# First expert layer of a graph kernel: transposes and node products at other places in TensorE's order, LayerNorm rows remade by ScalarE, an output norm in fused operations

## The chip, the core and the metric

The kernel runs on one core of a Trainium2 chip. The metric is the device time in microseconds of one execution, the median of three runs. A core has TensorE (PE in the profile, its weight loads PEld), VectorE (DVE), ScalarE (ACT), GpSimd (POOL) and SyncE (SP), which issues DMAs. Each engine runs its own instructions in the order in which they are written, and engines wait for one another by semaphores.

## What is computed

A graph layer and an expert layer, each twice, over 6250 nodes of 256 numbers. The part that matters is the first expert layer, and the first step of the second graph layer behind it:

```python
def _L0_ffn_ref(x, Wr, br, W1, b1, W2, b2, gamma, beta):
    ...
    h = jax.nn.gelu(jnp.einsum('nd,edf->enf', xf, W1) + b1[:, None, :], approximate=False)
    y = jnp.einsum('enf,efd->end', h, W2) + b2[:, None, :]
    ...
    out = jnp.einsum('ne,end->nd', w_dense, y).reshape(B, S, D)
    out = _layer_norm(out + x, gamma, beta)
    return out

def _L1_gnn_ref(x, W, edge_index):
    ...
    h = x @ W
    ...

x = x + _L0_gnn_ref(_layernorm(x, axis=-1), ...)
x = x + _L0_ffn_ref(_layernorm(x, axis=-1)[None], ...)[0]
x = x + _L1_gnn_ref(_layernorm(x, axis=-1), L1_gnn_W, edge_index)
```

All nodes share one choice of two experts, so the two experts together are one network with 1024 hidden units. Its input is LN1, the LayerNorm of x. Its result plus LN1 is normed with gamma and beta (the output norm) and added to x. LN2, the LayerNorm of that new x, is multiplied by the 256x256 matrix of the second graph layer, which gives the node products h.

## The kernel before

The 6250 rows are 50 tiles of P = 125 rows, taken GT = 2 at a time, so there are G = 25 groups g of N = 250 rows. Every engine has a function `ffn0(g)` that says what it does in its round g, and `in_turns` calls it for 0 to 24: the first few and the last few written out, the others in a hardware loop of two rounds a turn. Nothing but the order in these functions and the semaphores sets the order of the work. A float32 matrix product is made of three products of rounded parts: every operand is split into a high part and what is left (`h_hi`, `h0_lo`, `xB_hi`, `xB_lo`).

For one group the work runs through the engines like this:

- TensorE, `hidden0(g)`: the first products, in four quarters of 12 matmuls (L2088 to L2090), into four PSUM banks.
- ScalarE, `hidden0(g)`: two Gelu activations for each quarter (L794), and the high part `h_hi` of the quarter before (L787).
- GpSimd, `hidden0_lo(g)`: the low part of each quarter (L1028), four subtractions.
- TensorE, inside `ffn0(g)`: the second products, 48 matmuls (L2111 to L2113).
- VectorE, `ffn0(g)`: remakes the LN1 rows out of x with the kept mean and rstd (L1531), adds the bias `b2B` (L1535) and the products (L1538); statistics of y (L1406, L1411, L1413); GpSimd's `root` gives rstd (L998, semaphores `s_vB` and `s_rB`); then the norm (L1545), times gamma (L1547), plus beta (L1549), onto x (L1551); statistics of x; a second `root` (`s_v2`, `s_r2`); the LN2 rows `xh` (L1559).
- TensorE, `T2(g)`: four transposes of `xh` (L2067). ScalarE, `T2_copy(g)`: the copy into SBUF (L772). TensorE, `H(g)`: the node products (L2076).
- ScalarE, `h_copy(g)`: four activations (L780, L781) that write `h_row` and the high half of `h_part_r`. GpSimd, `h_lo_part(g)`: one subtraction (L1032) for the low half. SyncE, `store_h(g)`: the two stores to memory, of 256,000 bytes (L538) and 512,000 bytes (L539).

`h_row` and `h_part_r` exist once. So `h_copy(g)` waits until the stores of group g-1 have landed (the semaphores `h_written0` and `h_written1`, `s_hw` in the code):

```python
def h_copy(g, s):
    act.wait_ge(s_hm, g + 1)
    if not (isinstance(g, int) and g == 0):
        for k in range(2):
            act.wait_ge(s_hw[k], g * 16)
```

The rounds overlap. In round g TensorE does `T2(g-2)`, `hidden0(g+1)`, `H(g-2)` and the second products of g; ScalarE does `T2_copy(g-2)`, `hidden0(g+1)`, `x_hi(g+3)` and `h_copy(g-2)`; GpSimd does the root for the output norm of g-1, the four subtractions of g+1, the root for LN2 of g-1, and `h_lo_part(g-2)`. After the last round come two more `T2` and `H`, two `h_copy` and two `h_lo_part`. The next stage starts when the last stores and three loads behind them on SyncE's queue have landed.

Of the kernel before, what the change touches and what calls it, by code (L numbers as in the profile page):

```python
# [109 lines left out]
def build(nc, a, out):  # L110
# [3 lines left out]
    with ctx:  # L114
# [90 lines left out]
        b2B = b2A  # L205
        gamma = sb("gamma", [P, D])
# [196 lines left out]
        s_vB, s_rB = sem("lnB_var"), sem("lnB_rstd")  # L403
        s_v2, s_r2, s_x2, s_t2, s_t2e = sem("ln2_var"), sem("ln2_rstd"), sem("ln2_rows"), sem("ln2_T_in_psum"), sem("ln2_T_in_sbuf")
# [218 lines left out]
        def _(act):  # L623
# [139 lines left out]
            act.wait_ge(s_wbc, 1)  # L763
            act.wait_ge(s_wB, 96)
# [46 lines left out]

            for k in range(2):
# [142 lines left out]
        def _(pool):  # L955
# [78 lines left out]
            def ffn0(g, s=None):  # L1034
# [119 lines left out]
        def _(dve):  # L1154
# [299 lines left out]
            ln1_rows(G - 1, (G - 1) % 2)  # L1454

# [66 lines left out]
            def ffn0(g, s=None):  # L1522
# [15 lines left out]
                v.tensor_tensor(y, ps[0:P, 4 + s, :].rearrange("p (t d) -> p t d", t=GT), z, ALU.add).then_inc(s_oBe, 1)  # L1538
# [778 lines left out]
```

## Time and profile before

| | us |
|---|---|
| three runs | 3173.44, 3174.09, 3176.77; median 3174.09 |
| the profiled execution: its time, its span | 3175.92, 3174.1 |
| first expert layer's loop and its end (about 1496 to 1932 us of the span) | 436 |
| of the span busy: PE, PEld, DVE, ACT, POOL | 72%, 66%, 64%, 27%, 65% |
| mean granted clock of TensorE over the span | 0.826 |

A timeline row gives the start in us from the span's start, how long it took in us, the engine, the line, the operation, output and inputs, how many instructions stand in the row, and in brackets how long the engine had been idle and what ended that. A row of several instructions reads from the first one's start to the last one's end; matmuls and activations overlap their neighbours by a little, so the distance from start to start is what one costs. A row of a line "A:B" is a stretch of time with the busy time of each engine (and instructions), the granted clock as a share of full speed, the busy share of the DMA engines and GB/s.

### The profile page before, as it was taken

What the parts mean: (1) busy time and instruction counts of PE and PEld (TensorE: products, weight loads), DVE (VectorE), ACT (ScalarE), POOL (GpSimd) and SP (SyncE); (2) the same over time, 40 slices, a digit from 0 to 9 for tenths busy, and PEclk for the clock granted to TensorE, in tenths of its full rate; (3) what the DMA queues carried; (4) which work ended last, traced back from release to release, by engine and by line L of the source; (5) the groups of instructions that cost most, each with busy time, mean ns of one, the idle gap of its engine ahead of it and who ended that gap; (6) DMA issues with size and microseconds to landing.
All of it is one profiled execution on the core that took longest, in us unless ns stands there. A gap on an engine that the chain in (4) does not pass through costs nothing.

```text
span 3174.1 us, 49123 instructions
## 1 busy us (share of the span) xinstructions
PE 2284.6 (72%) x14349; PEld 2096.1 (66%) x14350; DVE 2044.1 (64%) x3305; ACT 863.4 (27%) x2246; POOL 2067.8 (65%) x1707
## 2 busy tenths in 40 slices
PE   0000047779899995997889984777887877798997
PEld 0000036668888885775889873666676767798997
DVE  8889976732323332465788876765665567488987
ACT  0000012210000000132545442344454421354543
POOL 5777877777777775010555545567788742488886
PEclk9999998865555555698999996899999895699999
DMA  6543345455444452122011114566777753423231
GB/s 202 151 115 94 81 124 152 146 163 123 114 114 117 113 136 71 50 77 66 20 49 51 51 61 139 140 165 187 193 197 190 192 146 112 86 63 84 63 90 33
DMA packets 341517, 358.60 MB, mean 113 GB/s; under 512 B 209280, under 2 KB 248560, under 8 KB 341125
## 3 DMA queue, kind: packets, MB, share of 16 engines
q1 hardware_dynamic: 209538, 196.84, 21.3%
q0 software_dynamic: 105984, 93.52, 13.0%
q10 hardware_dynamic: 25853, 66.46, 6.8%
q8 instruction: 75, 1.23, 0.2%
q14 instruction: 67, 0.55, 0.1%
HBM read 234.90 MB, written 122.85 MB: 113 GB/s over the span
## 4 chain that ended last, share of the span: by engine, by line
PE 35%; POOL 25%; issue 15%; DVE 13%; DMA 4%; DVEq 4%; SPq 4%; ACT 1%; another core or an unknown queue 0%; POOLq 0%; ACTq 0%
POOL sorted L989 18%; PE ps L1984 13%; PE ps L2133 4%; POOL h_lo L1028 3%; PE ps L2033 3%; PE ps L2152 3%; PE ps L2143 3%; DVEq L1596 2%; DVE hT L1606 2%; DVE yb L1874 2%; PE ps L2011 2%; POOL rstd L998 1%; SPq L595 1%; SPq L594 1%; DMA big<-x_rows,idx_a 1%
## 5 line engine op out<-in xcount | busy, mean ns | idle before, releaser
L1064 POOL DMA_INDIRECT mid<-h_rows,idx_a x400 | 485.5, 1214 | 172.5 <-issue 113.7
L1984 PE MATMUL ps<-big 128*128 128x65 f32 x2380 | 528.6, 419 | 87.5 <-issue 49.7
L1984 PEld LDWEIGHTS ps<-big 128*128 128x128 f32 x2380 | 514.0, 331 | 103.2 <-issue 102.4
L1361 DVE COPY mid<-big 128x28 f32 (+1 forms) x85 | 22.6, 266 | 448.2 <-PE ps L1984 306.8
L998 POOL TENSOR_TENSOR rstd<-var,neg_half 125x2 f32<-125x2 f32 (+1 forms) x75 | 63.2, 843 | 373.1 <-DVE var L1413 373.0
L989 POOL DMA_INDIRECT sorted<-yb,idx_a x200 | 239.6, 1198 | 83.9 <-issue 60.5
L989 POOL DMA_INDIRECT sorted<-wk,idx_a x200 | 238.1, 1191 | 60.9 <-issue 60.9
L989 POOL DMA_INDIRECT sorted<-xh,idx_b x200 | 237.9, 1190 | 60.9 <-issue 60.6
L989 POOL DMA_INDIRECT sorted<-mid,idx_b x200 | 237.9, 1190 | 60.9 <-issue 60.3
L2152 PE MATMUL ps<-adj,h_in_r 128*128 128x304 f32 (+3 forms) x980 | 244.2, 376 | 38.3 <-issue 36.1
L1606 DVE TENSOR_TENSOR hT<-ps,mid 128x608 bf16<-128x608 f32 (+3 forms) x245 | 255.1, 1041 | 0.1
L1897 PE MATMUL ps<-ones,ends 125*49 125x1 f32 x16 | 2.6, 230 | 343.5 <-DVE ends L1214 343.5
L2143 PE MATMUL ps<-hT,mid 128*128 128x288 bf16 (+3 forms) x637 | 146.2, 335 | 130.7 <-DVE hT L1606 108.7
L1897 PEld LDWEIGHTS ps<-ones,ends 125*49 125x49 f32 x16 | 1.9, 177 | 347.2 <-DVE ends L1214 332.0
L2133 PEld LDWEIGHTS ps<-mid 125*128 125x128 f32 x1600 | 218.8, 217 | 2.3 <-issue 1.5
L2152 PEld LDWEIGHTS ps<-adj,h_in_r 128*128 128x128 f32 x980 | 173.8, 212 | 68.6 <-issue 53.1
L2133 PE MATMUL ps<-mid 125*128 125x96 f32 x1600 | 216.9, 298 | 1.2 <-issue 1.2
L847 ACT ACTIVATE adj<-ps 128x304 fp32r<-128x304 f32 (+3 forms) x245 | 111.1, 457 | 373.4 <-PE ps L2143 276.3
L1598 DVE TENSOR_TENSOR mid<-hT,mid 128x2 f32<-128x2 f32 (+3 forms) x294 | 45.8, 161 | 217.0 <-PE ps L2143 107.5
L1107 POOL TENSOR_TENSOR h_lo<-x,h_hi 128x500 fp32r<-128x500 f32 x128 | 166.3, 1328 | 24.8 <-ACT h_hi L913 22.4
L1028 POOL TENSOR_TENSOR h_lo<-ends,h_hi 128x500 fp32r<-128x500 f32 x100 | 142.4, 1440 | 50.5 <-ACT h_hi L787 48.1
L1362 DVE TENSOR_TENSOR big<-ps,big 128x1792 f32<-128x1792 f32 x85 | 171.5, 2018 | 0.0
(333 smaller groups left out, 6534.4 us busy)
## 6 DMA issues: line engine op xcount, KB each, us to landing
h_in_r<-h_parts SPq DMA_DIRECT2D x245, 256.0 KB
big<-sorted ACTq DMA_DIRECT2D x85, 469.0 KB
sorted<-hT SPq DMA_DIRECT2D x73, 469.0 KB
mid<-in_L_ffn_w SPq DMA_DIRECT2D x16, 1024.0 KB
hid_x<-hT ACTq DMA_DIRECT2D x25, 500.0 KB
mid<-hid_x SPq DMA_DIRECT2D x25, 500.0 KB
h_parts<-h_part_r SPq DMA_DIRECT2D x25, 500.0 KB
mid<-h_rows,idx_a POOLq DMA_INDIRECT x400
```

The lines of the kernel that those rows point to most:

```text
L847: act.activation(adj[:, s, 0:w], ps[:, 2 + s, 0:w], ACT.Copy).then_inc(s_adje, 1)
L989: nc.gpsimd.indirect_dma_start(sorted_rows[c], bass.IndirectOffsetOnAxis(to_row[k][:, i:i + 1], 0), va[k][:, i, :], None).then_inc(s_put[k ...
L1028: nc.gpsimd.tensor_tensor(h0_lo[:, s, m, :], h0_whole[:, s, m, :], h_hi[:, s, m, :].bitcast(f32), ALU.subtract).then_inc(s_hBlo, 1)
L1064: nc.gpsimd.indirect_dma_start(mg4[:, s, i, :], None, h_rows, bass.IndirectOffsetOnAxis(idx4[:, s, i:i + 1], 0)).then_inc(s_gk[s], 16)
L1107: nc.gpsimd.tensor_tensor(h_lo[:, s, m, :], h_whole[:, m, :], h_hi[:, s, m, :].bitcast(f32), ALU.subtract).then_inc(s_hlo, 1)
L1362: v.tensor_tensor(node_hot[:, s % 2], lo_near.unsqueeze(1).to_broadcast([BR, GA, BR]), rows2[:, s, :, CW:CW + 1].to_broadcast([BR, GA, BR] ...
L1606: v.tensor_tensor(dst_sel[:, s, 0:n * w].rearrange("p (k w) -> p k w", w=w), near[:, 0:w].unsqueeze(1).to_broadcast([BR, n, w]), dst_rel[: ...
L1984: i_ = mm(banks[:, bass.ds(o_, CW)], node_hot[:, s % 2, i, :], rows2[:, s, i, 0:CW], start=False, stop=True, skip_group_check=True)
L2033: i_ = mm(ps[0:P, 4 + s, t * D:(t + 1) * D], hT[:, s, m, t * P:(t + 1) * P], wA2[:, m, :], start=(m == 0), stop=(m == 3))
L2133: i_ = mm(ps[:, 4 + s, c * WN:(c + 1) * WN], mg4[:, slot, i, c * 128:(c + 1) * 128], onto[:, slot, i, :], start=(i == 0), stop=(i == HW - 1))
L2143: i_ = mm(ps[:, 2 + s, 0:w], node_sel[:, s, k, :], dst_sel[:, s, k * w:(k + 1) * w], start=(k == 0), stop=(k == n - 1))
L2152: i_ = mm(ps[:, c, 0:w], h_in_r[:, slot, k, c * 128:(c + 1) * 128], adj[:, s, 0:w], start=(first and k == 0), stop=(last and k == 1))
```

## The change

It has five parts, all in the rounds of `ffn0`.

1. TensorE does `T2(g-2)` behind `hidden0(g+1)` rather than ahead of it, and `H(g-2)` behind the second products of g rather than ahead of them.
2. ScalarE's order follows: `hidden0(g+1)`, `T2_copy(g-2)`, the new `ln1_again(g+1)`, `x_hi(g+3)`, `h_copy(g-2)`.
3. ScalarE remakes the LN1 rows: `ln1_again` makes two Identity activations with the rstd as scale and minus mean times rstd as bias (`ln1_bias`, set once by VectorE in the storage of `cnt`), into `yb`. VectorE only adds `b2B` there, and then the products.
4. VectorE adds beta to x before it waits for the root; after it come two fused operations of 125x256, (y - mean) * gamma, and two, z * rstd + x, in the place of L1545 to L1551.
5. GpSimd does its subtraction for the stores one round later and in another place: `h_lo_part(g-3)` between the second and the third quarter of `hidden0_lo(g+1)`, where `h_lo_part(g-2)` came last in the round.

```diff
@@ ScalarE
+            def ln1_again(g, s):
+                if not (isinstance(g, int) and g < 2):
+                    act.wait_ge(s_yr, g - 1)
+                for t in range(GT):
+                    n = bass.ds(g * GT + t, 1)
+                    i_ = act.activation(yb[:, s, t, :], x[:, n, :].rearrange("p a d -> p (a d)"), ACT.Identity, bias=ln1_bias[:, n], scale=rstd1[:, n])
+                i_.then_inc(s_z, 1)
...
+                if not (fixed and g == G - 1):
+                    hidden0(g + 1, 1 - s)
                 if not (fixed and g < 2):
                     T2_copy(g - 2, s)
                 if not (fixed and g == G - 1):
-                    hidden0(g + 1, 1 - s)
+                    ln1_again(g + 1, 1 - s)
                 if not (fixed and g >= G - 3):
                     x_hi(g + 3, 1 - s)
                 if not (fixed and g < 2):
                     h_copy(g - 2, s)
@@ GpSimd
                 if not (fixed and g == G - 1):
-                    hidden0_lo(g + 1, 1 - s, range(4))
+                    hidden0_lo(g + 1, 1 - s, range(2))
+                if not (fixed and g < 3):
+                    h_lo_part(g - 3)
+                if not (fixed and g == G - 1):
+                    hidden0_lo(g + 1, 1 - s, range(2, 4))
                 if not (fixed and g == 0):
                     root(s_v2, s_r2, g, rstd2[:, 1 - s, :], var2[:, 1 - s, :])
-                if not (fixed and g < 2):
-                    h_lo_part(g - 2)
@@ VectorE
-                for t in range(GT):
-                    v.tensor_scalar(z[:, t, :], x[:, bass.ds(g * GT + t, 1), :].rearrange("p a d -> p (a d)"),
-                                    mv1[:, bass.ds(g * GT + t, 1), 0:1].rearrange("p a d -> p (a d)"),
-                                    rstd1[:, bass.ds(g * GT + t, 1)], ALU.subtract, ALU.mult).then_inc(s_dve, st.up())
-                settle()
-                v.tensor_tensor(z, z, wide(b2B), ALU.add).then_inc(s_dve, st.up())
+                dve.wait_ge(s_z, g + 1)
+                v.tensor_tensor(y, y, wide(b2B), ALU.add).then_inc(s_dve, st.up())
...
+                v.tensor_tensor(xs, xs, wide(beta), ALU.add).then_inc(s_dve, st.up())
                 dve.wait_ge(s_rB, g + 1)
                 for t in range(GT):
-                    v.tensor_scalar(z[:, t, :], y[:, t, :], mv[:, s, t, 0:1], rstd[:, s, t:t + 1], ALU.subtract, ALU.mult).then_inc(s_dve, st.up())
-                settle()
-                v.tensor_tensor(z, z, wide(gamma), ALU.mult).then_inc(s_dve, st.up())
-                settle()
-                v.tensor_tensor(z, z, wide(beta), ALU.add).then_inc(s_dve, st.up())
-                settle()
-                v.tensor_tensor(xs, xs, z, ALU.add).then_inc(s_dve, st.up())
+                    i_ = v.scalar_tensor_tensor(z[:, t, :], y[:, t, :], mv[:, s, t, 0:1], gamma[:, :], ALU.subtract, ALU.mult)
+                i_.then_inc(s_yr, 1)
...
+                    v.scalar_tensor_tensor(row, z[:, t, :], rstd[:, s, t:t + 1], row, ALU.mult, ALU.add).then_inc(s_dve, st.up())
@@ TensorE
-                if not (fixed and g < 2):
-                    T2(g - 2, s)
                 if not (fixed and g == G - 1):
                     hidden0(g + 1, 1 - s)
                 if not (fixed and g < 2):
-                    H(g - 2, s)
+                    T2(g - 2, s)
...
                 i_.then_inc(s_oB, 1)
+                if not (fixed and g < 2):
+                    H(g - 2, s)
```

The order of the instructions on GpSimd shows part 5. Here are the rounds that are written out behind the loop, before the change; `h_lo<-ends,h_hi` is a quarter of `hidden0_lo`, `h_part_r<-wk,h_part_r` is `h_lo_part`, the waits lnB_var and ln2_var belong to the two roots:

```order
L998 TENSOR_TENSOR rstd<-var,neg_half 125x2 [waits lnB_var]
L1028 TENSOR_TENSOR h_lo<-ends,h_hi 128x500 [waits ffn0_hidden_hi] x4
L998 TENSOR_TENSOR rstd<-var,neg_half 125x2 [waits ln2_var]
L1032 TENSOR_TENSOR h_part_r<-wk,h_part_r 125x2x256 [waits h_in_sbuf]
L998 TENSOR_TENSOR rstd<-var,neg_half 125x2 [waits lnB_var]
```

The same place with the change:

```order
L1012 TENSOR_TENSOR rstd<-var,neg_half 125x2 [waits lnB_var]
L1042 TENSOR_TENSOR h_lo<-ends,h_hi 128x500 [waits ffn0_hidden_hi] x2
L1046 TENSOR_TENSOR h_part_r<-wk,h_part_r 125x2x256 [waits h_in_sbuf]
L1042 TENSOR_TENSOR h_lo<-ends,h_hi 128x500 [waits ffn0_hidden_hi] x2
L1012 TENSOR_TENSOR rstd<-var,neg_half 125x2 [waits ln2_var]
L1012 TENSOR_TENSOR rstd<-var,neg_half 125x2 [waits lnB_var]
```

The subtraction for the stores stood behind the second root and all four quarters; it now stands behind two quarters of the next group.

On ScalarE the place is the end of one round and the start of the next, at the first rounds that have an `h_copy` (`wk` and `h_part_r` are its outputs, `xB_hi` is `x_hi`, `xTg` is `T2_copy`, `ends<-ps,bB` a Gelu). Before:

```order
L768 ACTIVATE xB_hi<-big 128x500 [waits ffn0_hidden_in_psum]
L780 ACTIVATE wk<-ps,dis 125x256 [waits h_in_psum]
L781 ACTIVATE h_part_r<-ps,dis 125x256
L780 ACTIVATE wk<-ps,dis 125x256
L781 ACTIVATE h_part_r<-ps,dis 125x256
L772 ACTIVATE xTg<-ps 128x500 [waits ln2_T_in_psum]
L794 ACTIVATE ends<-ps,bB 128x250 [waits ffn0_hidden_in_psum,ffn0_out_in_psum]
```

And with the change:

```order
L772 ACTIVATE xTg<-ps 128x500 [waits ln2_T_in_psum]
L805 ACTIVATE yb<-x,cnt,rstd 125x256 [waits ffn0_rows_read]
L805 ACTIVATE yb<-x,cnt,rstd 125x256
L768 ACTIVATE xB_hi<-big 128x500 [waits ffn0_hidden_in_psum]
L780 ACTIVATE wk<-ps,dis 125x256 [waits h_in_psum]
L781 ACTIVATE h_part_r<-ps,dis 125x256
L780 ACTIVATE wk<-ps,dis 125x256
L781 ACTIVATE h_part_r<-ps,dis 125x256
L794 ACTIVATE ends<-ps,bB 128x250 [waits ffn0_hidden_in_psum,ffn0_out_in_psum]
```

`T2_copy` has moved behind the hidden quarters, `ln1_again` (L805) has come in, and `h_copy` is still the last thing of a round, straight ahead of the next group's first Gelu.

## Rows read from the trace of the kernel before

**Rows 1.** Busy time by stretch: the rounds, a stretch with stores, one at half clock.
```profile
1496.00:1890.00 394.00, 349.05 (x2684) 339.09 (x2685) 312.17 (x536) 199.21 (x445) 214.12 (x171) 0.95 0.15 48
...
1604.00:1612.00 8.00, 7.76 (x61) 7.57 (x61) 6.93 (x14) 5.56 (x13) 3.89 (x4) 1.00 0.29 95
...
1637.00:1640.00 3.00, 3.00 (x16) 3.00 (x15) 2.51 (x7) 0.83 (x2) 0.85 (x1) 0.50 0.32 97
```

**Rows 2.** Who waited for whom, 1496 to 1890: total us, times, longest.
```profile
PE ps L2067 <- DVE xh L1559: 32.1, 18, 2.3
DVE xh L1559 <- POOL rstd L998: 26.9, 24, 1.9
...
DVE wk L1545 <- POOL rstd L998: 14.6, 24, 0.8
```

**Rows 3.** Timeline of VectorE: the addition of the products, twenty rounds apart.
```profile
1542.87 0.69 DVE L1538 TENSOR_TENSOR yb<-ps,wk 125x512 f32<-125x512 f32 x1
...
1850.82 0.69 DVE L1538 TENSOR_TENSOR yb<-ps,wk 125x512 f32<-125x512 f32 x1
```

**Rows 4.** VectorE's groups in 1542.8 to 1850.7: count, busy us, mean ns, idle before.
```profile
L1547 DVE TENSOR_TENSOR wk<-wk,gamma 125x512 f32<-125x512 f32 x20 | 29.3, 1463 | 0.7
...
L1535 DVE TENSOR_TENSOR wk<-wk,b2A 125x512 f32<-125x512 f32 x21 | 14.5, 693 | 0.7
L1531 DVE TENSOR_SCALAR wk<-x,mv,rstd 125x256 f32 x40 | 14.5, 403 | 0.0
```

**Rows 5.** Timeline of TensorE: second products, transposes, first products, node products.
```profile
1540.26 0.28 PE L2113 MATMUL ps<-wB_hi,h_lo 128*125 128x256 f32 x1
1541.51 0.65 PE L2067 MATMUL ps<-ident,xh 125*128 125x125 f32 x4 [0.97 <-DVE xh L1559]
1541.92 0.36 PE L2088 MATMUL ps<-xB_hi,wB_hi 128*128 128x250 f32 x1
...
1547.62 1.89 PE L2076 MATMUL ps<-wG,xTg 128*125 128x256 f32 x8
1549.16 0.47 PE L2111 MATMUL ps<-wB_hi,h_hi 128*125 128x256 f32 x1
...
1554.92 0.28 PE L2113 MATMUL ps<-wB_hi,h_lo 128*125 128x256 f32 x1
```

**Rows 6.** Timeline of GpSimd: quarters and the subtraction ahead of the stores.
```profile
1617.87 1.26 POOL L1032 TENSOR_TENSOR h_part_r<-wk,h_part_r 125x512 fp32r<-125x512 f32 x1
...
1847.57 1.28 POOL L1032 TENSOR_TENSOR h_part_r<-wk,h_part_r 125x512 fp32r<-125x512 f32 x1
...
1855.73 1.25 POOL L1028 TENSOR_TENSOR h_lo<-ends,h_hi 128x500 fp32r<-128x500 f32 x1 [0.15 <-ACT h_hi L787]
...
1877.79 1.30 POOL L1032 TENSOR_TENSOR h_part_r<-wk,h_part_r 125x512 fp32r<-125x512 f32 x1
```

**Rows 7.** Timeline of SyncE: the issue of the second store of one group.
```profile
1849.49 0.32 SPq L539 DMA_DIRECT2D h_parts<-h_part_r  x1
```

**Rows 8.** Timeline of ScalarE: starts of h_copy (L780), and a stretch without waits.
```profile
1520.32 1.55 ACT L794 ACTIVATE ends<-ps,bB 128x250 f32<-128x250 f32 x4
...
1522.99 0.62 ACT L787 ACTIVATE h_hi<-ends 128x500 fp32r<-128x500 f32 x1
...
1550.08 0.47 ACT L780 ACTIVATE wk<-ps,dis 125x256 f32<-125x256 f32 x1
...
1628.21 0.48 ACT L780 ACTIVATE wk<-ps,dis 125x256 f32<-125x256 f32 x1
1628.58 0.47 ACT L781 ACTIVATE h_part_r<-ps,dis 125x256 fp32r<-125x256 f32 x1
...
1857.78 0.48 ACT L780 ACTIVATE wk<-ps,dis 125x256 f32<-125x256 f32 x1 [0.19 <-DMA h_parts<-h_part_r]
...
1874.89 0.47 ACT L780 ACTIVATE wk<-ps,dis 125x256 f32<-125x256 f32 x1
...
1888.05 0.47 ACT L780 ACTIVATE wk<-ps,dis 125x256 f32<-125x256 f32 x1 [6.52 <-DMA h_parts<-h_part_r]
...
1901.14 0.47 ACT L780 ACTIVATE wk<-ps,dis 125x256 f32<-125x256 f32 x1 [10.05 <-DMA h_parts<-h_part_r]
```

More of the change, by code:

```diff
@@ L205, in build @@
         b2B = b2A
+        ln1_bias = cnt
         gamma = sb("gamma", [P, D])
@@ L403, in build @@
         s_vB, s_rB = sem("lnB_var"), sem("lnB_rstd")
+        s_lnb, s_z, s_yr = sem("ln1_bias_set"), sem("ln1_rows_again"), sem("ffn0_rows_read")
         s_v2, s_r2, s_x2, s_t2, s_t2e = sem("ln2_var"), sem("ln2_rstd"), sem("ln2_rows"), sem("ln2_T_in_psum"), sem("ln2_T_in_sbuf")
@@ L760, in _ @@
             act.activation(rt[:, 11, 0:2], rt[:, 10, 0:2], ACT.Exp, accum_out=rt[:, 9, 4:5]).then_inc(s_e1x, 1)
-            act.wait_ge(s_wbc, 1)
-            act.wait_ge(s_wB, 96)
             def x_hi(g, s):
@@ L810, in ffn0 @@
                     h_copy(g - 2, s)
+            act.wait_ge(s_lnb, 1)
+            ln1_again(0, 0)
+            act.wait_ge(s_wbc, 1)
+            act.wait_ge(s_wB, 96)
             for k in range(2):
@@ L1039, in ffn0 @@
                 if not (fixed and g == G - 1):
-                    hidden0_lo(g + 1, 1 - s, range(4))
+                    hidden0_lo(g + 1, 1 - s, range(2))
[3 more added lines that the diff above has]
+                    hidden0_lo(g + 1, 1 - s, range(2, 4))
                 if not (fixed and g == 0):
                     root(s_v2, s_r2, g, rstd2[:, 1 - s, :], var2[:, 1 - s, :])
-                if not (fixed and g < 2):
-                    h_lo_part(g - 2)
             hidden0_lo(0, 0, range(4))
-            in_turns(pool, steps, ffn0, G, 2, 3, 2)
+            in_turns(pool, steps, ffn0, G, 4, 3, 2)
             root(s_vB, s_rB, G, rstd[:, (G - 1) % 2, :], var[:, (G - 1) % 2, :])
+            h_lo_part(G - 3)
             root(s_v2, s_r2, G, rstd2[:, (G - 1) % 2, :], var2[:, (G - 1) % 2, :])
@@ L1454, in _ @@
             ln1_rows(G - 1, (G - 1) % 2)
+            settle()
+            v.scalar_tensor_tensor(ln1_bias[:, :], mv1[:, :, 0:1].rearrange("p t a -> p (t a)"), -1.0, rstd1[:, :], ALU.mult, ALU.mult).then_inc(s_lnb, 1)
             dve.wait_ge(s_t1e, G)
@@ L1529, in wide @@
                     return r[:, :].unsqueeze(1).to_broadcast([P, GT, D])
-                for t in range(GT):
-                    v.tensor_scalar(z[:, t, :], x[:, bass.ds(g * GT + t, 1), :].rearrange("p a d -> p (a d)"),
-                                    mv1[:, bass.ds(g * GT + t, 1), 0:1].rearrange("p a d -> p (a d)"),
-                                    rstd1[:, bass.ds(g * GT + t, 1)], ALU.subtract, ALU.mult).then_inc(s_dve, st.up())
-                settle()
-                v.tensor_tensor(z, z, wide(b2B), ALU.add).then_inc(s_dve, st.up())
+                dve.wait_ge(s_z, g + 1)
+                v.tensor_tensor(y, y, wide(b2B), ALU.add).then_inc(s_dve, st.up())
                 settle()
                 dve.wait_ge(s_oB, g + 1)
-                v.tensor_tensor(y, ps[0:P, 4 + s, :].rearrange("p (t d) -> p t d", t=GT), z, ALU.add).then_inc(s_oBe, 1)
+                v.tensor_tensor(y, ps[0:P, 4 + s, :].rearrange("p (t d) -> p t d", t=GT), y, ALU.add).then_inc(s_oBe, 1)
                 dve.wait_ge(s_oBe, g + 1)
@@ L1542, in ffn0 @@
                     x_lo(g + 3, 1 - s)
+                v.tensor_tensor(xs, xs, wide(beta), ALU.add).then_inc(s_dve, st.up())
                 dve.wait_ge(s_rB, g + 1)
                 for t in range(GT):
-                    v.tensor_scalar(z[:, t, :], y[:, t, :], mv[:, s, t, 0:1], rstd[:, s, t:t + 1], ALU.subtract, ALU.mult).then_inc(s_dve, st.up())
+                    i_ = v.scalar_tensor_tensor(z[:, t, :], y[:, t, :], mv[:, s, t, 0:1], gamma[:, :], ALU.subtract, ALU.mult)
+                i_.then_inc(s_yr, 1)
+                dve.wait_ge(s_yr, g + 1)
                 settle()
-                v.tensor_tensor(z, z, wide(gamma), ALU.mult).then_inc(s_dve, st.up())
-                settle()
-                v.tensor_tensor(z, z, wide(beta), ALU.add).then_inc(s_dve, st.up())
-                settle()
-                v.tensor_tensor(xs, xs, z, ALU.add).then_inc(s_dve, st.up())
+                for t in range(GT):
+                    row = x[:, bass.ds(g * GT + t, 1), :].rearrange("p a d -> p (a d)")
+                    v.scalar_tensor_tensor(row, z[:, t, :], rstd[:, s, t:t + 1], row, ALU.mult, ALU.add).then_inc(s_dve, st.up())
                 settle()
```

## The prediction

> **What bounds the kernel now.** I read only the stage that the change touches, 436 us of the span, and started with its busy times: TensorE is at work for 349 of 394 us and the granted clock averages 0.95 [rows 1], so it has gaps, though small ones. The waits name them: it sat 32.1 us waiting for VectorE's LN2 rows ahead of the transposes, about 2 us each time, and VectorE in turn waited 26.9 and 14.6 us for GpSimd's roots [rows 2]. Then the timeline of VectorE: from the addition of the products in one group to that in another, twenty rounds later, are 1850.82 - 1542.87 = 307.95 us, 15.40 us a round [rows 3], and VectorE never waits for the products there. So the ring VectorE, root, VectorE, root, VectorE sets the round of **15.4 us**. It is long because its operations run beside GpSimd's subtractions: the gamma product takes 1463 ns where the equal-sized addition of b2B, with GpSimd idle, takes 693 [rows 4].
>
> TensorE alone would need less. By the starts [rows 5] the transposes take 0.41, the first products 5.70, the node products 1.54 and the second products 5.75 us (1549.16 to about 1554.9): **13.4 us** at full clock.
>
> A third ring hardly shows. h_row and h_part_r exist once, so ScalarE's h_copy of a group waits for the stores of the group before. In one round GpSimd's subtraction ended at 1847.57 + 1.28 = 1848.85 [rows 6], the second store was issued at 1849.49 [rows 7], and h_copy began at 1857.78, released by that store [rows 8]: 8.93 us. A second case: 1877.79 + 1.30 = 1879.09 to 1888.05, 8.96 us [rows 6, 8]. Inside the loop this wait is just missed: subtraction done at 1617.87 + 1.26 = 1619.13, landing expected at 1628.06, h_copy at 1628.21 [rows 6, 8]. Only 0.15 us of slack. That makes this ring the first thing to check in the change.
>
> **The change, part by part.** *VectorE.* Gone are two row operations of 403 ns and, in place of a pair of norm operations and three of 512 columns, there are four fused ones of 256 columns and one addition of 512, the latter under the wait for the root. The trace has no fused operation of this shape with all inputs in SBUF; bounds are 0.4 us each alone (the 256-column form of L1531) and 0.9 beside GpSimd (twice that, as gamma shows) [rows 4]. With 0.4, VectorE's own work is five additions of some 0.69, three pairs of 0.75 for the fused operations and the LN2 rows, and two sets of statistics of 1.2: 3.4 + 2.3 + 2.4 = 8 us, with gaps and two root waits about 11; with all six 256-column operations at 0.9, about 14. I take the lower, because in the new order VectorE is waiting for the second root while GpSimd subtracts. Against the forecast's round of 16.5 either end costs nothing.
>
> *ScalarE* gets two activations of 125x256 a round, 0.36 us each by the spacing of the same shape (1628.21 to 1628.58 [rows 8]); its round holds some 10 us of work, so this costs nothing. The first ones fall into its idle time before the weights come, and the one small VectorE operation for the bias is hidden there too.
>
> *TensorE.* The transposes have 5.70 us more until they are due, and the node products have the second products between them and the transposes. That takes away its 2 us gaps if the rows come in time; they will.
>
> *GpSimd and the stores.* This is where I expect the time to go. Count one ScalarE round from the start of h_copy of group k. Its four activations need 1.43 us; the next Gelus and splits follow at once, since in ScalarE's order the next hidden0 comes straight behind. From the first Gelu to the end of the second quarter's split is 1522.99 + 0.62 - 1520.32 = 3.29 us where ScalarE never waits [rows 8]. Then GpSimd: 0.07 to the start and 1.25 for that quarter [rows 6], 0.1 for the first quarter still ahead of it, 0.12 between instructions, 1.28 for the subtraction of group k [rows 6]. Then 8.93 us until the stores have landed [rows 6 to 8], and only now may h_copy of group k+1 start. Sum: 1.43 + 3.29 + 0.07 + 1.25 + 0.1 + 0.12 + 1.28 + 8.93 = **16.5 us a round**, against 15.4. Before, the path from h_copy to the subtraction had no hidden work of the next group in it. Bounds: 16.35 without the small gaps, 16.8 with both GpSimd operations slowed to the 1.4 us that they take beside VectorE. The wait sits on ScalarE; queued behind it are the Gelus of the next group, and behind those GpSimd's quarters and the second products. TensorE has finished the first products long before (8.3 us after h_copy it leaves the node products, at 14 it has all four quarters in PSUM), so it is TensorE that then idles, about 3 us a round.
>
> In the Trainium skill, the page "DMA: Bandwidth & Descriptors" (section "Anatomy of one DMA — SWDGE (gpsimd) path") fits one DMA of the GpSimd path as about 2.0 us plus its bytes at 436 GB/s. By that fit the 768,000 bytes of both stores would land in 3.8 us and the ring would be 11.3 us, below TensorE's 13.4: the change would then be the gain of the second case below. The trace disagrees for these stores, which SyncE issues, with 8.93 and 8.96 us.
>
> **The sum.** First h_copy: TensorE ends the second products of group 1 at 1540.3 [rows 5]; now follow 5.70 + 0.41 + 5.75 and 1.89 for the node products, so it starts at 1554.2, not 1550.08 [rows 8]. From there to h_copy of group 21 are 21 rounds (the ring holds from the second h_copy on): 1554.2 + 21 x 16.5 = 1900.7. The next one has no hidden quarters ahead of the subtraction: 1.56 + 0.1 + 1.28 + 8.93 = 11.9, so 1912.6. Before it started at 1888.05 [rows 8]. From that point both kernels do the same: h_copy, subtraction, stores, 13.09 us to the next [rows 8], then the loads of the next stage. The difference is 1912.6 - 1888.05 = **+24.5 us**. The profiled execution took 3175.9 and would be 3200.4; the median of the runs, 3174.1, is 1.8 us lower, and from it the time is 3198.6. I say **3199**. With 16.35 and 16.8 us a round it would be 3195 and 3205, and some 5 us on each side go to the two ends of the stage.
>
> **Rivals.** *The stores land in time (faster).* Place: the wait ahead of h_copy. It needs a landing in under 13.4 - 7.6 = 5.8 us. Then TensorE bounds with 13.4 us: 1554.2 + 21 x 13.4 + 11.9 = 1847.5, 40.5 us earlier than now, 3133.5 us. For it: the DMA engines are busy only 29% while the stores run [rows 1], so something other than their number is the limit. Against: nothing in the change touches the stores' size or queue, and two waits in the trace give 8.9.
>
> *No change.* The landing would have to be about 7.8 us, or VectorE's ring would have to stay at 15.4 with the stores hidden. The round stays as it is, 3174. Nothing in the rows speaks for it.
>
> *TensorE's clock falls (slower still).* Where a gap of 2.3 us came before the transposes, a stretch at clock 0.50 followed, at 1637 to 1640 [rows 1]. Its gap now grows to some 3 us a round. One such stretch costs TensorE about 1.7 us, which the 3 us hide. It decides only when the mean granted clock falls under 13.4 / 16.5 = 0.81; at 0.7 a round is 19.1 us and the time 3199 + 21 x 2.6 = 3254. Against it: 0.95 in this stage so far.
>
> *The change doesn't do what it says* isn't open: the printed orders show each part.
>
> **How the numbers follow.** The forecast's case 0.84; stores in time 0.07; no change 0.03; clock 0.06. A measurement of this kernel can tell about 0.2%, 6.3 us, from no change. The first and last cases are slower by more: slower 0.90, same 0.03, faster 0.07. The range is the forecast's own bounds with the ends of the stage, 3190 to 3210; it holds nearly all of the 0.84.
>
> **What would show it.** In the new profile ScalarE's h_copy must wait for the DMA of h_part_r in nearly every round, some 8 us each, over 150 us in all; the distance from one h_copy to the next must be 16.5 us; TensorE's wait for the LN2 rows must be gone, with a gap ahead of the node products, released by ScalarE's copy, in its place; VectorE must wait longest for the second root. If h_copy doesn't wait, the ring was wrong; if it waits and the round is still under 15.4, the stores landed faster than 8.9 us; if the round is right and the end is off, it was the last three h_copy.

## The result

The changed kernel takes 3195.64 us (median of 4 runs, 3194.15 to 3197.53) against 3175.43 (4 runs, 3173.44 to 3180.54). The ratio is 1.0065, interval 1.005 to 1.008: it is slower, as forecast, by some 20 us. The profiled spans are 3195.4 and 3174.1 us. A "round" below is the distance from one h_copy of the loop to the next; the "stage" runs from the first activation that splits `wB` to the first `idx_a` activation of the next stage. The round grew from 15.4 to 16.35 us and the stage from 425.8 to 447.9.

First the busy times of the stage after the change (columns as in [rows 1]: stretch, its length, PE, PEld, DVE, ACT, POOL busy with counts, clock, DMA share, GB/s):

```profile
1496.00:1910.00 414.00, 357.05 (x2687) 343.18 (x2688) 198.43 (x504) 213.50 (x494) 196.90 (x172) 0.93 0.13 44
```

VectorE's busy time fell from 312 us [rows 1] to 198: it has less to do, and more of its work runs while GpSimd is idle (in experiment 1 below, where it runs beside GpSimd, the same work is 280 us). TensorE idles for 57 us now, 45 before. The waits of the same stretch (total us, times, longest) tell where the gain went:

```profile
ACT wk L780 <- DMA h_parts<-h_part_r: 175.9, 22, 9.8
DVE xh L1575 <- POOL rstd L1012: 171.4, 24, 8.4
...
POOL rstd L1012 <- DVE var L1430: 91.6, 26, 3.9
PEld ps L2092 <- ACT xTg L772: 50.5, 20, 8.9
PE ps L2092 <- ACT xTg L772: 46.3, 20, 8.7
```

ScalarE waits 22 times, 8 us each, for the second store; in the kernel before it waited for it twice in 1496 to 1890, 6.7 us in all. VectorE now waits 171 us for the root of LN2, where it waited 27 [rows 2]. TensorE's 32 us of waiting for LN2 rows [rows 2] are gone, and 46 us of waiting for ScalarE's copy of the transposed rows stand in their place, ahead of the node products.

One round of ScalarE, from one h_copy (L780) to the next; this is the ring itself (start, duration, what ended the idle time before):

```profile
1699.98 0.47 ACT L780 ACTIVATE wk<-ps,dis 125x256 f32<-125x256 f32 x1 [7.92 <-DMA h_parts<-h_part_r]
...
1701.43 1.56 ACT L794 ACTIVATE ends<-ps,bB 128x250 f32<-128x250 f32 x4
1702.83 0.67 ACT L787 ACTIVATE h_hi<-ends 128x500 fp32r<-128x500 f32 x1
...
1706.74 1.17 ACT L805 ACTIVATE yb<-x,cnt,rstd 125x256 f32 x2
1707.72 0.69 ACT L768 ACTIVATE xB_hi<-big 128x500 fp32r x1
1716.39 0.47 ACT L780 ACTIVATE wk<-ps,dis 125x256 f32<-125x256 f32 x1 [7.97 <-DMA h_parts<-h_part_r]
```

GpSimd in the same round: two quarters, the subtraction, two quarters.

```profile
1703.58 2.49 POOL L1042 TENSOR_TENSOR h_lo<-ends,h_hi 128x500 fp32r<-128x500 f32 x2 [4.73 <-ACT h_hi L787]
1706.03 1.26 POOL L1046 TENSOR_TENSOR h_part_r<-wk,h_part_r 125x512 fp32r<-125x512 f32 x1
1707.25 2.47 POOL L1042 TENSOR_TENSOR h_lo<-ends,h_hi 128x500 fp32r<-128x500 f32 x2
```

And SyncE, which issues the two stores:

```profile
1707.48 0.26 SPq L540 DMA_DIRECT2D h_rows<-wk  x1
1707.93 0.32 SPq L541 DMA_DIRECT2D h_parts<-h_part_r  x1
```

Read together: h_copy starts at 1699.98; the first Gelu follows at 1701.43; GpSimd waits until the first quarter has been split and then needs two quarters before it reaches the subtraction at 1706.03, which ends at 1707.29; the stores leave at once; ScalarE, whose own work is over at 1708.4, starts the next h_copy at 1716.39. That is 6.05 + 1.26 + 9.10 = 16.41 us.

### The profile page after: what moved, and what is told of

Same layout as the page of the kernel before. It is cut to its first block, busy times and chain, and to the rows that moved or that the text cites. A ratio compares the mean times of both kernels' runs of the same rounds, so it can differ in the third digit from the quotient of the medians.

```text
span 3195.4 us, 49127 instructions
## 1 busy us (share of the span) xinstructions
PE 2293.3 (72%) x14349; PEld 2102.3 (66%) x14350; DVE 1927.4 (60%) x3256; ACT 876.8 (27%) x2296; POOL 2044.6 (64%) x1707
## 4 chain that ended last, share of the span: by engine, by line
POOL 30%; PE 27%; issue 18%; DVE 12%; DMA 6%; SPq 4%; DVEq 2%; ACT 1%; POOLq 0%; ACTq 0%
POOL sorted L1003 20%; PE ps L2000 11%; POOL mid L1081 4%; PE ps L2149 3%; PE ps L2049 3%; POOL h_lo L1042 2%; DMA h_parts<-h_part_r 2%; DVE yb L1890 2%; PE ps L2027 2%; PE ps L2168 1%; SPq L597 1%; SPq L596 1%; POOL rstd L1012 1%; DVE hT L1622 1%; DVEq L1612 1%
## 5 line engine op out<-in xcount | busy, mean ns | idle before, releaser
L2149 PE MATMUL ps<-mid 125*128 125x96 f32 x1600 | 227.6, 307 | 36.3 <-issue 18.2
L1042 POOL TENSOR_TENSOR h_lo<-ends,h_hi 128x500 fp32r<-128x500 f32 x100 | 124.7, 1265 | 130.6 <-ACT h_hi L787 129.8
```

What stands on the lines that cost most here:

```text
L1042: nc.gpsimd.tensor_tensor(h0_lo[:, s, m, :], h0_whole[:, s, m, :], h_hi[:, s, m, :].bitcast(f32), ALU.subtract).then_inc(s_hBlo, 1)
L2149: i_ = mm(ps[:, 4 + s, c * WN:(c + 1) * WN], mg4[:, slot, i, c * 128:(c + 1) * 128], onto[:, slot, i, :], start=(i == 0), stop=(i == HW - 1))
```

## The experiments

The theory: part 5, the early subtraction, closes a ring h_copy, first two quarters, subtraction, stores, h_copy. The rivals: it is the landing of the stores whatever the order; it is the new order on TensorE and ScalarE (parts 1 and 2); or the fused operations cost what was lost. Runs are given with their ratio to the kernel before on the same chip. The chips differ in the whole (the kernel before took 3271 us beside the first four, 3173 beside the next four, 3259 beside the last three), so times of different chips aren't set side by side, only ratios, rounds and stages. Rounds and stages come from one profiled execution each.

| kernel | ratio (interval) | round | stage |
|---|---|---|---|
| before | 1 | 15.4 | 425.8 |
| changed | 1.0065 (1.005 to 1.008) | 16.35 | 447.9 |
| 1 changed, subtraction last | 0.9866 (0.984 to 0.9893) | 13.46 | 386.4 |
| 2 changed, one quarter later | 1.0112 (1.0082 to 1.0142) | 17.57 | 473.3 |
| 3 before with part 5 | 1.0104 (1.0075 to 1.0134) | 16.87 | 463.4 |
| 4 changed, first store early | 0.9893 (0.9867 to 0.992) | 14.1 | 396.1 |
| 5 before with parts 3, 4 | 0.9866 (0.9848 to 0.9883) | 13.43 | 381.6 |
| 6 before with parts 1, 2 | 1.0021 (1.001 to 1.0032) | 15.5 | 429.1 |
| 7 = 1 and 4 together | 0.9852 (0.9835 to 0.9869) | 13.46 | 383.9 |
| 8 = 1, first store from ScalarE's queue | 0.9843 (0.9826 to 0.9859) | 13.46 | 383.9 |
| 9 = 5 with first store early | 0.9858 (0.9835 to 0.9881) | 13.43 | 376.7 |
| 10 = 9, big load from ScalarE's queue | 0.9849 (0.9826 to 0.9872) | 13.43 | 380.5 |
| 11 changed, again | 1.0076 (1.0051 to 1.01) | 16.35 | 447.1 |

The 16.35 us of the changed kernel is the mean of 21 rounds, the first of which took 17.0; without it a round is 16.32. The rounds of the experiments are without the first ones. A whole-kernel ratio and the stage agree only to within some 10 us: in experiment 2 the stage is 47.5 us longer than before and the whole 37, in 4 the stage 30 shorter and the whole 35. What a change is worth in a round is therefore read from rounds and stages, and the ratios say only which way and about how far the whole goes.

### 1: part 5 undone

```diff
-                    hidden0_lo(g + 1, 1 - s, range(2))
-                if not (fixed and g < 3):
-                    h_lo_part(g - 3)
-                if not (fixed and g == G - 1):
-                    hidden0_lo(g + 1, 1 - s, range(2, 4))
+                    hidden0_lo(g + 1, 1 - s, range(4))
                 if not (fixed and g == 0):
                     root(s_v2, s_r2, g, rstd2[:, 1 - s, :], var2[:, 1 - s, :])
+                if not (fixed and g < 2):
+                    h_lo_part(g - 2)
...
-            h_lo_part(G - 3)
```

> The changed kernel with part 5 alone undone: GpSimd's subtraction ahead of the stores stands last in its round again, with the group of that round. Store ring theory: h_copy, subtraction and landing are then 1.45 + 1.3 + 9.1, some 12 us, h_copy no longer waits for a DMA, TensorE bounds the round with 13.4 us, and 21 rounds are 62 us shorter: about 3130 us, faster than the kernel before by some 45. Rival A, the new places of the transposes and node products or ScalarE's longer round cost the time: the round stays near 16.4 and the time near 3195. Rival B, VectorE's ring is still the bound: about 3175.

Measured: 3225.3 us against 3271.48, ratio 0.9866, 46 us faster than the kernel before; a round of 13.46 us. The same stretch by busy time (columns as above):

```profile
1536.00:1875.00 339.00, 329.67 (x2637) 323.85 (x2638) 279.87 (x476) 217.78 (x489) 201.03 (x167) 0.98 0.16 51
```

TensorE is at work for 97% of it. The waits, 1540 to 1870:

```profile
ACT wk L780 <- PE ps L2089: 89.0, 21, 4.6
POOL h_part_r L1046 <- ACT h_part_r L781: 66.3, 21, 4.4
```

ScalarE's h_copy now waits for the node products, and in this stretch never for a store. What part 5 undone brings, 447.9 - 386.4 = 61.5 us of the stage, is the cost of part 5 in the changed kernel: the ring's 16.35 against TensorE's own round, 21 times 2.9, is 61. GpSimd in one round:

```profile
1794.62 1.28 POOL L1046 TENSOR_TENSOR h_part_r<-wk,h_part_r 125x512 fp32r<-125x512 f32 x1 [3.00 <-ACT h_part_r L781]
1796.00 1.06 POOL L1012 TENSOR_TENSOR rstd<-var,neg_half 125x2 f32<-125x2 f32 x1
1797.04 5.48 POOL L1042 TENSOR_TENSOR h_lo<-ends,h_hi 128x500 fp32r<-128x500 f32 x4
```

The subtraction stands directly behind the h_copy it belongs to, and the hidden quarters come after it, so their time runs while the stores land.

### 2: the subtraction one quarter later

```diff
-                    hidden0_lo(g + 1, 1 - s, range(2))
+                    hidden0_lo(g + 1, 1 - s, range(3))
...
-                    hidden0_lo(g + 1, 1 - s, range(2, 4))
+                    hidden0_lo(g + 1, 1 - s, range(3, 4))
```

> The changed kernel with the subtraction one quarter later, behind the third quarter rather than the second. Store ring theory: the ring grows by one GpSimd quarter, 1.25 us (one ScalarE quarter, 1.2 to 1.4 us), so a round is 17.6 to 17.8 us and the time 3195.6 + 21 x 1.25 to 1.4, 3222 to 3225 us. Rival, the round is set by TensorE or VectorE: no difference, 3195 us.

Measured: 3309.06 us, ratio 1.0112, a round of 17.57 us. The stage grew by 473.3 - 447.9 = 25.4 us, as forecast (21 x 1.25 = 26); the whole is 38 us slower than before where 47 to 50 were forecast. One round of GpSimd:

```profile
1799.94 3.70 POOL L1042 TENSOR_TENSOR h_lo<-ends,h_hi 128x500 fp32r<-128x500 f32 x3 [5.96 <-ACT h_hi L787]
1803.59 1.28 POOL L1046 TENSOR_TENSOR h_part_r<-wk,h_part_r 125x512 fp32r<-125x512 f32 x1
```

and the h_copy on either side of it:

```profile
1796.34 0.48 ACT L780 ACTIVATE wk<-ps,dis 125x256 f32<-125x256 f32 x1 [9.12 <-DMA h_parts<-h_part_r]
...
1813.98 0.48 ACT L780 ACTIVATE wk<-ps,dis 125x256 f32<-125x256 f32 x1 [9.19 <-DMA h_parts<-h_part_r]
```

Without the first rounds, the round grew by 17.57 - 16.32 = 1.25 us; one quarter is 2.49 / 2 = 1.25. The quarter put ahead of the subtraction is paid in full. Had TensorE or VectorE set the round, this edit would have changed nothing.

### 3: part 5 alone on the kernel before

The diff is the reverse of experiment 1's, made to the kernel before (with four rounds of GpSimd written out ahead of its loop and not two, as in the changed kernel); parts 1 to 4 are absent.

> The kernel before with part 5 alone: everything in the old order, but the subtraction ahead of the stores one round later, behind the second quarter. Store ring theory: the same ring as in the changed kernel plus what stands in ScalarE's old order ahead of the Gelus (the copy of the transposes, 0.5 us) and GpSimd slowed by VectorE's longer work: 16.9 to 17.6 us a round against 15.4, so some 35 to 50 us slower than before, 3208 to 3225 us. Rival A (the new TensorE order costs the time): as before, 3175 us.

Measured: 3300.34 us, ratio 1.0104, a round of 16.87 us. Waits, 1560 to 1870:

```profile
ACT wk L780 <- DMA h_parts<-h_part_r: 150.2, 16, 9.7
```

The wait appears without any of the other parts: part 5 is enough. The loss is 29 us by the medians, 34 by the ratio and 38 in the stage, so at or under the low end of the 35 to 50 expected, and the round is just under its range of 16.9 to 17.6; the slower VectorE ring of the old code (15.4) and the stores' ring don't add, the longer one sets the round. The 0.55 us between 16.87 and the changed kernel's 16.32 are, for the most part, the copy of the transposes, which in the old order stands between h_copy and the first Gelu:

```profile
1739.11 0.47 ACT L780 ACTIVATE wk<-ps,dis 125x256 f32<-125x256 f32 x1 [9.40 <-DMA h_parts<-h_part_r]
...
1740.55 0.61 ACT L772 ACTIVATE xTg<-ps 128x500 f32<-128x500 f32 x1
1741.02 1.58 ACT L794 ACTIVATE ends<-ps,bB 128x250 f32<-128x250 f32 x4
```

The first Gelu comes 1.91 us behind h_copy, where it was 1.45, and the subtraction 6.52 us behind it (it starts at 1745.63), where it was 6.05. The landing is the same, 9.13 us to the next h_copy at 1756.05. GpSimd slowed by VectorE, the other reason that was expected, doesn't show: two quarters take 2.49 us here too.

### 4: the first store ahead of the subtraction

```diff
-                sp.wait_ge(s_hplo, HPLO + g + 1)
+                sp.wait_ge(s_hrow, g + 1)
                 sp.dma_start(h_v[:, bass.ds(g * GT, GT), :], h_row).then_inc(s_hw[0], 16)
+                sp.wait_ge(s_hplo, HPLO + g + 1)
```

The store of h_row doesn't need the subtraction, only h_copy.

> The changed kernel, with the first store (h_rows, a third of the bytes) issued as soon as h_copy is done and only the second one behind the subtraction. Store ring theory, if the landing follows the bytes: 9.1 us become about 6.3, the ring 13.6 us, just over TensorE's 13.4; the time 3195.6 - 21 x 2.8 and some 6 us at the stage's end: about 3132 us. If the landing is mostly a fixed delay rather than bytes: 8 us or more remain, 3165 to 3185 us. Rival (TensorE's order or the clock bounds): 3195 us.

Measured: 3236.67 us, ratio 0.9893, a round of 14.1 us (13.6 expected). The end of the ring in one round, first GpSimd's subtraction, then SyncE's stores, then ScalarE's h_copy (L781 in this kernel):

```profile
1861.52 1.28 POOL L1047 TENSOR_TENSOR h_part_r<-wk,h_part_r 125x512 fp32r<-125x512 f32 x1
```

```profile
1857.21 0.26 SPq L540 DMA_DIRECT2D h_rows<-wk  x1
1862.96 0.26 SPq L542 DMA_DIRECT2D h_parts<-h_part_r  x1
```

```profile
1869.57 0.47 ACT L781 ACTIVATE wk<-ps,dis 125x256 f32<-125x256 f32 x1 [6.17 <-DMA h_parts<-h_part_r]
```

From the subtraction's end, 1862.80, the landing takes 6.77 us instead of 9.10; the ring is 6.05 + 1.28 + 6.77 = 14.1 us, still above TensorE's 13.4. So the bytes behind the subtraction count, 256,000 of them for 2.3 us. The miss of 0.5 us is the landing: 6.3 was assumed. The ratio, 35 us faster than before, misses the expected 3132 us (43 faster) by 8.

### 5 and 6: the other parts, in two halves

Experiment 6 is the kernel before with parts 1 and 2 only, the new orders (`T2` and `H` of TensorE as in the diff of the change):

```diff
@@ ScalarE
-                if not (fixed and g < 2):
-                    T2_copy(g - 2, s)
                 if not (fixed and g == G - 1):
                     hidden0(g + 1, 1 - s)
+                if not (fixed and g < 2):
+                    T2_copy(g - 2, s)
@@ TensorE
-                if not (fixed and g < 2):
-                    T2(g - 2, s)
                 if not (fixed and g == G - 1):
                     hidden0(g + 1, 1 - s)
                 if not (fixed and g < 2):
-                    H(g - 2, s)
+                    T2(g - 2, s)
...
+                if not (fixed and g < 2):
+                    H(g - 2, s)
```

Experiment 5 is the other half: the changed kernel with these two pieces and part 5 put back, so parts 3 and 4 alone on the old orders of all three engines.

> The kernel before with parts 3 and 4 alone (ScalarE remakes the LN1 rows, VectorE's fused norm); TensorE's and ScalarE's old order and the subtraction in its old place. Theory: VectorE's ring of 15.4 us is what bounded before, and its shortening alone gives the whole gain of about 2 us a round: the transposes are ready in time even at the head of the round, TensorE bounds with 13.4 us, 42 to 50 us faster than before. Rival: the old order still makes TensorE wait for the LN2 rows, and the new places are needed: a round of 14.5 to 15 us, 10 to 20 us faster.

Measured: 3134.21 us against 3173.08, ratio 0.9866, a round of 13.43 us; the stage is 44 us shorter than before. Busy times, 1540 to 1815:

```profile
1540.00:1815.00 275.00, 275.00 (x2214) 270.38 (x2213) 212.84 (x414) 182.58 (x412) 173.54 (x143) 1.00 0.17 56
```

TensorE has no gap left in 275 us, at full clock. With the LN1 rows remade by ScalarE and the norm fused, VectorE's ring falls below TensorE's 13.4 us without any step of TensorE being moved.

> The kernel before with parts 1 and 2 alone (transposes behind the first products, node products behind the second, ScalarE's copy behind its hidden quarters); VectorE's and GpSimd's work as before. Theory: VectorE's ring does not pass through TensorE, so the round stays 15.2 to 15.5 us and only the first h_copy comes some 4 us later: the time within 0.2% of before (0 to +6 us), TensorE's wait moves from the transposes to another place. Rival, the order itself gains or costs: 10 us or more either way.

Measured: 3179.49 us (10 runs), ratio 1.0021, interval 1.001 to 1.0032. Waits, 1540 to 1850:

```profile
POOL rstd L998 <- DVE var L1413: 137.9, 40, 4.4
ACT wk L780 <- DMA h_parts<-h_part_r: 103.5, 16, 6.7
PE ps L2067 <- DVE xh L1559: 29.3, 18, 1.9
...
DVE xh L1559 <- POOL rstd L998: 17.1, 20, 0.9
```

TensorE waits for LN2 rows as before (29 us, [rows 2] has 32): the new places take nothing away as long as VectorE sets the round. The wait for the stores shows here too. In one round the root of LN2, which waits for VectorE, ends at 1707.2, the subtraction behind it at 1708.5, and h_copy starts at 1717.46, 9.0 us later. The stores follow VectorE here and don't set the round: GpSimd waits for VectorE ahead of both roots of every round (137.9 us, 40 times in the 20 rounds), and VectorE waits for nothing but these roots (17.1 us, and 11.8 at L1545). The forecast, 0 to 6 us slower, is met at its edge, with 6.4 by the medians. In the stage the loss is 3.3 us: the first h_copy comes 47.55 us after the stage's start and not 43.67, 3.9 us later, as was forecast.

### 7 to 10: is there more to have at the end of the stage?

Behind the loop two stores and a load of 1.2 MB still stand in the way. Experiment 7 is 1 and 4 together. Experiment 8 sends the first store from ScalarE's own queue:

```diff
@@ h_copy
+                act.wait_ge(s_hrow, g + 1)
+                act.dma_start(h_v[:, bass.ds(g * GT, GT), :], h_row).then_inc(s_hw[0], 16)
@@ SyncE
-                sp.dma_start(h_v[:, bass.ds(g * GT, GT), :], h_row).then_inc(s_hw[0], 16)
```

> The changed kernel with both: the subtraction last in GpSimd's round with the group of that round, and the first store issued as soon as h_copy is done. Theory: the loop is bound by TensorE at 13.4 us in either case, so the early store gains only in the chain of the last three h_copy, 2.3 us for each of three: 5 to 8 us faster than the same kernel without the early store, which was 46 us faster than before: ratio to before 0.984. Rival, the stores still count in the loop: 20 us or more.

> As the run before, but the first store is issued by ScalarE on its own queue straight behind h_copy. Theory: the same loop of 13.4 us; ScalarE has about 3 us of idle time a round, so the issue is hidden there; the end of the stage gains the same 5 to 8 us. If the two queues also move bytes side by side, nothing more is to be seen since the stores do not overlap. Rival: ScalarE's wait for its own copies delays the next Gelus by 0.3 to 1 us a round and costs 6 to 20 us against the run before.

Measured: 3127.08 and 3126.79 us against 3173.08; the two are the same, and 1 alone has 0.9866 where they have 0.985 (the intervals overlap). The round is TensorE's, so an earlier store saves only at the stage's end, 386.4 to 383.9 us. That is 2.5 us where 5 to 8 were forecast: of the last three distances between h_copies, 12.4, 13.0 and 15.1 us in 1, only the first two shrank, to 11.3 and 11.6, and the third, which has the load of 1.2 MB in it, stayed.

> The kernel before with parts 3 and 4 and the early first store, in the old order of TensorE and ScalarE. Theory: TensorE bounds the loop with 13.4 us as in the run with parts 3 and 4 alone, and the chain of the last h_copy is shorter by 5 to 8 us: 44 to 48 us faster than before, 3127 us, no worse than with the new places of transposes and node products. Rival, the new places gain something of their own: 5 us or more slower than the run with the subtraction last and the early rows.

Measured: 3213.23 us against 3259.37, ratio 0.9858, stage 376.7. Experiment 9 is 5 with experiment 4's edit. By the stage it is the shortest of all; by the ratio it can't be told from 5, 7 and 8. The early store is worth 4.9 us of the stage here, 381.6 to 376.7.

Experiment 10 takes the load of `ends` from SyncE, where it stands ahead of the stores of group 23, to ScalarE's queue behind an h_copy:

```diff
+                if fixed and g == G - 1:
+                    act.wait_ge(s_oB, G)
+                    act.dma_start(ends[0:P, 0:KEPT], ends_kept).then_inc(s_back, 16)
```

> As the run before, but the load of 1.2 MB that SyncE issues between the last stores comes from ScalarE's queue as soon as the last second products are done. The stores moved about 111 GB/s on SyncE's queue (256,000 bytes fewer landed 2.3 us sooner). If that is a limit of the queue, the two run side by side, the last two h_copy come 3 to 6 us sooner, and the time is 5 to 9 us less; if it is a limit of what the core's DMA engines move for such rows, the load only delays an earlier store and the gain is 0 to 3 us.

Measured: 3212.47 us, the same as 9. ScalarE at the end of the stage (the h_copy is L778 in this kernel):

```profile
1874.46 0.47 ACT L778 ACTIVATE wk<-ps,dis 125x256 f32<-125x256 f32 x1 [4.82 <-DMA h_parts<-h_part_r]
...
1877.41 0.29 ACTq L821 DMA_DIRECT2D ends<-ends_kept  x1
1894.32 0.47 ACT L778 ACTIVATE wk<-ps,dis 125x256 f32<-125x256 f32 x1 [15.29 <-DMA h_parts<-h_part_r]
```

The last two distances between h_copies are 19.9 and 10.2 us, 30.0 together, where 9 has 11.7 and 15.1, 26.7 together. The load moved by one group; the distance that it joined grew by 8.2 us and the one that it left shrank by 4.9, and the stage is 3.8 us longer, neither the gain of the first forecast (5 to 9 us) nor quite the second (0 to 3). The store issued beside the load, at 1877.58, landed 16.7 us later, at the next h_copy; in 9, with the load issued on the same queue just behind it, the same store took 8.7, and the one of experiment 4 with no load near it 6.6. A second queue doesn't let the load pass beside the stores: SyncE's queue by itself isn't the limit. While both are under way the row is this (columns as above):

```profile
1880.00:1890.00 10.00, 2.17 (x9) 1.28 (x8) 5.69 (x16) 0.00 (x0) 1.76 (x2) 0.74 0.33 135
```

The busy share of the 16 DMA engines is 0.33, as it is with the stores alone (0.33 in the changed kernel, 1710 to 1714, a row that stands near the end of the next section). One third of 16 is about five engines' worth, and two queues get no more of them than one. In other stages of the changed kernel the share reaches 0.7. What holds these transfers of 125 rows a time to a third was not tried.

### 11: the changed kernel on another chip

> The changed kernel as it is, on the chip of the two runs above. Theory: 20 us slower than before, a ratio of 1.0065; the round 16.35 us as in its first profile. Rival, the round depends on the chip: a ratio outside 1.004 to 1.009.

Measured: ratio 1.0076, round 16.35, stage 447.1 us, the same wait:

```profile
ACT wk L780 <- DMA h_parts<-h_part_r: 176.0, 22, 9.9
```

The stage takes the same on a chip where this kernel takes 89 us more (3284.26 against 3195.64), so on these two chips what is said of the stage doesn't hang on the chip.

## Why the prediction was right, step by step

**The bound before.** Right, and now by experiment: VectorE's ring set 15.4 us. Parts 3 and 4, which shorten it, bring TensorE's bound by themselves (experiment 5), 13.43 against the 13.4 worked out from [rows 5].

**The store ring.** Right in mechanism and place: h_copy waits for the second store 22 times, 175.9 us, where over 150 were forecast. By its terms, from the timelines above: h_copy to the subtraction's start 6.05 us, forecast 1.43 + 3.29 + 0.07 + 1.25 + 0.1 + 0.12 = 6.26; the subtraction 1.26 against 1.28; the landing 9.10 against 8.93 from [rows 6 to 8]. The 0.21 us too many are the two small gaps of 0.1 and 0.12, which the timeline doesn't have. The misses have opposite signs, so part of the closeness is luck, and 16.35 us measured over 21 rounds, (1895.72 - 1552.45) / 21, stands against 16.5. The starts are these:

```profile
1552.45 0.47 ACT L780 ACTIVATE wk<-ps,dis 125x256 f32<-125x256 f32 x1 [4.04 <-PE ps L2092]
...
1895.72 0.47 ACT L780 ACTIVATE wk<-ps,dis 125x256 f32<-125x256 f32 x1 [8.33 <-DMA h_parts<-h_part_r]
1907.52 0.47 ACT L780 ACTIVATE wk<-ps,dis 125x256 f32<-125x256 f32 x1 [9.75 <-DMA h_parts<-h_part_r]
```

**The sum.** The first h_copy came at 1552.45, 1.75 us ahead of the forecast's 1554.2; about 2.8 us of that is the stage having begun earlier (1503.60 against 1506.41), so against the stage's start it is 1 us late. The earlier start is no gain of the new LN1 rows: experiment 6, which doesn't have them, begins the stage at 1503.87. The rounds gave 0.15 us less each, 3.2 us in all. Group 21 to 22 took 11.80 us, forecast 11.9. The h_copy of group 22 is at 1907.52, forecast 1912.6: 1907.52 - 1888.05 = +19.5 us and not +24.5. The last h_copy is 19.4 us later than before, 1935.65 against 1916.21, and the span 21.3; the remaining 1.9 us lie behind this stage and I did not find their place. The terms that were mis-sized are the first h_copy, by the stage's earlier start, and the round, by 0.15 us; 3195.6 was measured, 3199 forecast.

**VectorE.** "With 0.4 to 0.9 each" was half right. Alone, a fused operation takes 0.48 us (groups of 1560 to 1880: count, busy us, mean ns, idle before):

```profile
L1561 DVE SCALAR_TENSOR_TENSOR wk<-yb,mv,gamma 125x256 f32<-125x256 f32 x40 | 17.6, 483 | 0.6 <-POOL rstd L1012 0.6
L1567 DVE SCALAR_TENSOR_TENSOR x<-wk,rstd,x 125x256 f32 x38 | 16.7, 482 | 2.3
```

In experiment 1, where they run beside GpSimd's subtractions, they take three times as long (1580 to 1850):

```profile
L1558 DVE SCALAR_TENSOR_TENSOR wk<-yb,mv,gamma 125x256 f32<-125x256 f32 x40 | 56.1, 1441 | 2.4 <-POOL rstd L1012 2.4
...
L1564 DVE SCALAR_TENSOR_TENSOR x<-wk,rstd,x 125x256 f32 x38 | 51.3, 1388 | 2.3
```

The upper bound, twice the duration alone as for the gamma product, was too low: 1.44 us is about what one GpSimd quarter takes there, 5.48 / 4 = 1.37, and that is what the gamma product took too [rows 4]. By these two sizes it isn't a factor but the length of the neighbour's operation. An operation with one input of this size does it as well: the norm's 125x256 (L1545) took 1.33 us beside the quarters in experiment 6 (at 1699.66), where the same shape takes 0.40 alone [rows 4]. That changed nothing here, because VectorE had the time in either case. In the Trainium skill, the page "SBUF — State Buffer" (section "Who interferes with whom") says that a VectorE instruction with two SBUF inputs contends with a GpSimd instruction that reads SBUF, and calls the lock exclusive; 0.48 us alone and 1.44 beside are in line with it. No run here separates the ports themselves.

**ScalarE.** The two activations of `ln1_again` take 0.98 us from start to start of what follows (1706.74 to 1707.72), 0.49 each and not the 0.36 of h_copy's. They are free, since ScalarE then waits 8 us. Its work in a round is 1708.41 - 1699.98 = 8.4 us, where the prediction said some 10.

**TensorE.** The gaps ahead of the transposes are gone, the one ahead of the node products came; both as forecast.

```profile
1706.99 1.99 PE L2092 MATMUL ps<-wG,xTg 128*125 128x256 f32 x8 [1.02 <-ACT xTg L772]
```

The clock fell only from 0.95 [rows 1] to 0.93, so that rival played no part.

**The landing, in two terms.** The prediction set beside its sum a fit of 2.0 us plus bytes at 436 GB/s, by which the change would gain. From experiment 4: 512,000 bytes land 1869.57 - 1862.96 = 6.61 us after their issue; both stores, 768,000 bytes, took 1716.39 - 1707.48 = 8.91 us after the first issue. The difference of 2.30 us for 256,000 bytes is 111 GB/s, and 6.61 - 4.60 leaves 2.0 us. In the Trainium skill, the page "DMA: Bandwidth & Descriptors" (section "Anatomy of one DMA — SWDGE (gpsimd) path") has that fixed part; its rate, of the GpSimd path, is four times what these stores, issued by SyncE, reach. Two points make a line in any case, and they are of two kernels, so the fixed part is an estimate. The rate shows in the trace itself, in the middle of one landing of the changed kernel:

```profile
1710.00:1714.00 4.00, 4.00 (x37) 4.00 (x36) 3.27 (x10) 0.00 (x0) 0.41 (x2) 1.00 0.33 112
```

That is 112 GB/s. No bytes move in 1716 to 1717, where h_copy begins.

**What the prediction left out.** That the other parts are worth 42 us by themselves: 386.4 against 425.8 is 39 us in the stage, and 0.9866 in the whole. The prediction came to that sum only in a rival, "the stores land in time", which has 40.5 us for a loop that TensorE bounds. It took this for a question of how fast stores land, with a chance of 0.07, and didn't say that the gain is to be had by leaving part 5 out. Part 5 costs 61.5 us on top of that.

## The better version

Experiments 5, 7, 8 and 9 beat both kernels, with ratios of 0.984 to 0.987. By time they can't be told apart; 5 is the simplest. It needs none of the moves of parts 1, 2 and 5, and in the stage the old order of TensorE and ScalarE is the shorter one, 381.6 against 386.4 us (5 and 1) and 376.7 against 383.9 (9 and 7).

## What to carry to other kernels

Before an instruction is moved, list the buffers that exist once and close the ring through them, with the landing of a DMA as one of its links: 0.15 us of slack was the only sign that a ring would be next. A step that feeds a store from such a buffer belongs directly behind what fills it; every operation put ahead of it is paid in full (1.25 us of the round for a quarter of 1.25). And a change with several parts is to be priced part by part: here one of them cost 61 us of the stage and hid the 39 that the others bring.

## What the runs showed of the hardware

- A VectorE operation with two inputs in SBUF takes 1.4 us beside GpSimd's subtractions, whether it is 125x256 (0.48 alone) or 125x512 (0.69 alone [rows 4]).
- Stores from 125 partitions issued by SyncE: about 2.0 us (an estimate from two landings, 6.61 and 8.91 us) and then some 111 GB/s. The busy share of the 16 DMA engines is 0.33 while they run, and 0.13 to 0.17 over the stage.
- A load of 1.2 MB issued from another engine's queue delayed the landing of the store beside it by 8 us (16.7 us, against 8.7 where the load came behind it on the same queue); the share of the DMA engines stayed at 0.33.
- On another chip the same kernel took 2.8% more (3284 against 3196), and the stage 447.1 us against 447.9.
